# Two-layer convolution block on one core: another order of layer 1's operations on all five engines

## The chip, the core and the metric

The kernel runs on one core of a Trainium2 chip. The metric is the device time of one execution in microseconds (us); lower is better. TensorE (PE) multiplies matrices, VectorE (DVE), ScalarE (ACT) and GpSimd (POOL) work elementwise, and SyncE (SP) issues all the DMAs of the part that is changed. Each engine takes its instructions in program order; they meet through semaphores (`wait_ge`, `then_inc`).

## What is computed

The input x is 4 images of 64 channels by 256 by 256, f32. Each layer adds to x a function of its group norm. Layer 0 (projection, depthwise convolution, patchwise Fourier product, layer norm, projection) is not touched. Layer 1, which is, is cut to this:

```python
xn   = group_norm(x)
r    = einsum('oc,bchw->bohw', w_reduce, xn) + b_reduce        # 64 -> 64
rn   = relu(batch_norm(r))
kern = einsum('kc,bchw->bkhw', w_span, rn) + b_span            # 9 taps for each pixel
inv  = einsum('bkhw,bckhw->bchw', kern, patches_3x3(xn))
z    = softplus(inv)
x    = x + softplus(conv3x3(z, w_conv2) + b_conv2)
```

## The kernel before, in words

Layer 1 runs over 132 strips of 8 image rows. A strip lies as 128 partitions (64 channels, twice, for even and odd rows) by 1024 elements (4 rows of 256). A loop of 33 rounds has four bodies each, k = 0 to 3; the first round is written out, since the first strips have no strips before them. In body k each engine works on several strips at once, as its own hand-written list says. With "strip k" for the body's own strip:

- TensorE, `body` in the block of `pe`. `select(n, b, j)` (line 1309, 2 matmuls) spreads tap n of the kernel values over the 64 channels into one of two PSUM bank pairs; nine for each strip, of which taps 0 and 1 of strip k+1 stand at the end of body k. `r_product` (line 1314, twice) makes r of strip k+2, `weights` (line 1319) its 9 kernel values. `conv(b, h, products)` (line 1327) makes half h of the output convolution from 6 products, the line's records being two for a product. Half 1 has PSUM bank 7, and so do r, the kernel values and `k_rest`: these follow each other in that bank once a strip.
- VectorE. Nine multiplications `prod[n]` (line 1570; tap 7 goes straight to the PSUM pair `b_x`), `add_to_x` (line 1518) adds `prod[8]` and later GpSimd's sum `part_sum` to `b_x`, `z_finish` (line 1528) ends the first softplus, `rest` (1536) and `third_parts` (1541) split the kernel values into three bf16 parts, `residual` (1555, two halves) adds the input to the positive part of the convolution.
- GpSimd. Six additions (line 1292) sum `prod[0]` to `prod[6]` into `part_sum`; one addition (line 1299) makes the output `res`.
- ScalarE. The three normed copies of x, `x_mid` (from `xa`), `x_up` and `x_down` (from `xb`; lines 1397 and 1399), the absolute value, exp and log of both softplus functions, `bn_relu` (1443), the masked edge rows of z (1435, 1437), and two of the bf16 parts (`high_parts` 1451, `second_parts` 1456).
- SyncE. `stack_parts` (1213) writes the three parts to DRAM, `stack_back` (1218, six DMAs) brings them back as `kern_parts`, for `select`; `load_a`, `load_b` (1197 to 1203) load x and `store` (1207) writes the output.

The softplus is computed as max(v,0) + log(1 + exp(-|v|)).

## Time and profile before

| | |
|---|---|
| median of 3 runs | 10036.34 us (10029.1 to 10041.79) |
| profiled execution, its own time | 10034.93 us |
| its span | 10033.1 us, granted TensorE clock 0.988 on the mean |
| layer 1 in it | from about 7440 us to the end |

The trace was read for one strip out of layer 1's steady part, where each strip takes the same time. A row of the timeline has the start in us, the duration, the engine and line, the operation with what it writes and reads, and in brackets the idle time of the engine before it with what ended it. A duration is longer than the distance to the next start on VectorE and ScalarE, since an instruction begins as the one in front drains; a sum over an engine therefore goes by distances between starts.

### The profile page before, as it was taken

Reading aid. Unit: us, or ns where it says so; the run is one execution under the profiler, and the core shown is the slowest. Engines: PE = TensorE matmul, PEld = TensorE weight load, DVE = VectorE, ACT = ScalarE, POOL = GpSimd, SP = SyncE. Lnnn points to the kernel's source line nnn. Section 1 sums busy time; section 2 is a strip of 40 time slices with the busy share of each in tenths; the row PEclk is TensorE's granted clock in tenths of the full one; section 3 lists DMA queues with packets and bytes.
Section 4 is the critical chain, followed back from the end, with each engine's and each line's share of the span. In section 5 each row is a group of like instructions: output and inputs, shape, how many; then the busy total and the mean of one; then the engine's idle time right before and its main releaser. Section 6 shows DMA issues by size and latency. Waiting matters only on the chain. (4 is left out here: it accounts for less than half of the span.)

```text
span 10033.1 us, 169594 instructions
## 1 busy us (share of the span) xinstructions
PE 9128.4 (91%) x58854; PEld 5045.6 (50%) x58854; DVE 6036.7 (60%) x7784; ACT 6973.9 (70%) x9573; POOL 4896.1 (49%) x2751
## 2 busy tenths in 40 slices
PE   1999999999999999999999999999868888888888
PEld 0666666666666666666665555555322222222222
DVE  4555555555555555555555454544558888888887
ACT  1777777777777777777776767767217777777777
POOL 1334433343344344433433333333118888888888
PEclk9999999999999999999999999999989999999999
DMA  6122222222222222222212111111764444444444
GB/s 129 47 60 55 48 57 56 56 50 55 60 55 47 59 56 55 50 55 60 55 39 48 39 48 39 47 40 39 162 157 105 104 104 104 104 104 104 104 104 102
DMA packets 619184, 718.26 MB, mean 72 GB/s; under 512 B 44324, under 2 KB 578138, under 8 KB 595142
## 3 DMA queue, kind: packets, MB, share of 16 engines
q1 hardware_dynamic: 618950, 714.70, 30.2%
q8 instruction: 200, 3.28, 0.1%
q14 instruction: 34, 0.28, 0.0%
HBM read 549.65 MB, written 164.89 MB: 71 GB/s over the span
## 5 line engine op out<-in xcount | busy, mean ns | idle before, releaser
L550 PE MATMUL banks<-w_hi,hi_lo 128*128 128x256 f16 x18432 | 2380.6, 275 | 132.5 <-issue 80.9
L550 PEld LDWEIGHTS banks<-w_hi,hi_lo 128*128 128x128 f16 x18432 | 1795.2, 99 | 556.4 <-issue 209.9
L508 POOL TENSOR_TENSOR u_im<-q_im,k_swap 128x512 f32<-128x512 f32 x512 | 706.4, 1380 | 2136.2 <-ACT q_im L706 2082.8
L1292 POOL TENSOR_TENSOR part_sum<-part_sum,prod 128x1024 f32<-128x1024 f32 x660 | 1559.8, 2363 | 261.7 <-DVE prod L1570 218.8
L1327 PE MATMUL banks<-z,conv_w 128*128 128x512 f32 x3140 | 1523.4, 614 | 0.0
L688 ACT ACTIVATE qk<-banks,inv_wscale 128x512 f32<-128x512 f32 x1024 | 689.9, 687 | 1040.8 <-PE banks L550 1028.4
L818 DVE TENSOR_TENSOR u<-q_re,banks 128x512 f32<-128x512 f32 x512 | 351.0, 686 | 1717.1 <-ACT q_re L712 1341.5
L511 POOL TENSOR_TENSOR u<-u,u_im 128x512 f32<-128x512 f32 x512 | 649.7, 1269 | 1338.8 <-DVE u L818 1338.8
L567 PE MATMUL banks<-hi_lo,w_hi 128*128 128x512 f16 x4608 | 1085.7, 381 | 13.9 <-DVE tmp L887 13.9
L550 PE MATMUL banks<-w_lo_pair,hi_pair 128*128 128x256 f16 x6144 | 1012.0, 274 | 0.0
L498 POOL TENSOR_TENSOR hl_all<-xn,hi_all 64x1280 f16<-64x1280 f32 x258 | 793.2, 3074 | 241.2 <-ACT hi_all L681 219.2
L1327 PEld LDWEIGHTS banks<-z,conv_w 128*128 128x128 f32 x3140 | 540.6, 188 | 613.2 <-issue 613.2
L517 POOL TENSOR_TENSOR u<-u,u_mean 128x512 f32<-128x512 f32 x512 | 532.2, 1039 | 513.4 <-DVE u_mean L833 513.4
L567 PEld LDWEIGHTS banks<-hi_lo,w_hi 128*128 128x128 f16 x4608 | 431.0, 98 | 650.5 <-issue 209.9
L597 PEld LDWEIGHTS banks<-idft,u 128*128 128x128 f32 x4096 | 496.3, 191 | 511.8 <-issue 322.7
L696 ACT ACTIVATE v_s<-banks,inv_wscale 128x512 f32<-128x512 f32 x512 | 349.6, 683 | 546.4 <-PE banks L567 546.4
L675 ACT ACTIVATE xn<-xr,par 128x2816 f32<-128x2816 f32 x129 | 684.0, 5302 | 27.0 <-DMA xr<-in_x_dram 27.0
L1570 DVE TENSOR_TENSOR prod<-banks,x_up 128x1024 f32<-128x1024 f32 x396 | 482.6, 1219 | 313.6 <-PE banks L1309 313.6
L597 PE MATMUL banks<-idft,u 128*128 128x128 f32 x4096 | 594.0, 288 | 73.8 <-POOL u L517 73.8
L550 PEld LDWEIGHTS banks<-w_lo_pair,hi_pair 128*128 128x128 f16 x6144 | 604.3, 98 | 72.6
L1309 PE MATMUL banks<-kern_parts,sel 64*128 64x512 bf16 x2380 | 443.7, 388 | 196.8 <-DVE prod L1570 196.5
L831 DVE TENSOR_REDUCE u_mean<-u 128x4 f32<-128x512 f32 x512 | 351.0, 686 | 434.0 <-POOL u L511 434.0
(210 smaller groups left out, 16400.3 us busy)
## 6 DMA issues: line engine op xcount, KB each, us to landing
xr<-in_x_dram SPq DMA_DIRECT2D x258, 640.0 KB, 9.1
xb<-y_scratch SPq DMA_DIRECT2D x268, 320.0 KB, 4.8
xa<-y_scratch SPq DMA_DIRECT2D x270, 256.0 KB, 5.3
x_res<-in_x_dram SPq DMA_DIRECT2D x258, 256.0 KB, 4.2
out_dram<-res SPq DMA_DIRECT2D x258, 256.0 KB, 5.1
y_scratch<-ys SPq DMA_DIRECT2D x256, 256.0 KB, 4.1
yc<-y_scratch SPq DMA_DIRECT2D x256, 256.0 KB, 6.0
xs<-in_x_dram SPq DMA_DIRECT2D x92, 512.0 KB, 7.1
```

The source lines that it names most:

```text
L498: nc.gpsimd.tensor_tensor(hl_all[C:P, 1 + c0:1 + c1, 1:SL], xn[C:P, c0:c1, 0:SL - 1], hi_all[C:P, 1 + c0:1 + c1, 0:SL - 1], ALU.subtract). ...
L508: nc.gpsimd.tensor_tensor(u_im[:], q_im[:], k_swap[:], ALU.mult).then_inc(u_made, 1)
L511: nc.gpsimd.tensor_tensor(u[:], u[:], u_im[:], ALU.add).then_inc(u_step, 1)
L517: nc.gpsimd.tensor_tensor(u4, u4, u_mean[:].unsqueeze(2).to_broadcast([P, 4, P]), ALU.subtract)\
L550: r = pe.matmul(out, px, w, start=n == 0, stop=n == 13)
L567: r = pe.matmul(b_v[:], w, px, start=n == 0, stop=n == 13)
L597: last = pe.matmul(by_patch[:, p, t], u[:, block], idft[:], start=True, stop=True)
L675: act.activation(xn[:, :, 0:SL], xr[b][:].rearrange("p s w -> p w s"), ACT.Identity, bias=par[b][:, 1:2], scale=par[b][:, 0:1]).then_inc(x ...
L688: act.activation(qk[:, 2 * h:2 * h + 2, :], b_qk[h][:].rearrange("p (t c) -> p t c", t=2), ACT.Copy, scale=inv_wscale[:, 0:1]).then_inc(qk ...
L1292: nc.gpsimd.tensor_tensor(part_sum[:], prod[0][:] if n == 0 else part_sum[:], prod[n + 1][:], ALU.add)\
L1327: last = pe.matmul(b_c[h][:], conv_w[:, n, :], z[b][:, 2 * h + j:2 * h + j + 2, dc:dc + W], start=n == 0, stop=n == 5)
L1570: v.tensor_tensor(by_row(to), by_row(flat(b_kern[(9 * k + n) % 2])), src[:, :, 1 + dc:1 + dc + W], ALU.mult).then_inc(prod_ready, 1)
```

## The change

The set of operations, their sizes and their tiles stay the same. What moves:

- TensorE: the convolution's half 0 is cut into products 0, 1, 2, 3 (each on its own behind a select or another product) and 4, 5; half 1 of the strip before goes from behind select 1 to behind selects 3, 4 and 6 of the next body. Both `r_product` go from behind selects 5 and 6 to behind selects 8 and 0, `weights` to behind select 1.
- VectorE: `rest`, `third_parts` and `add_to_x(prod[8])` go to behind tap 1 of the next body, `residual` to behind taps 4 and 6.
- GpSimd: the output addition of a strip is made one strip later, at the start of a body.
- ScalarE: `second_parts` and `norm_up` go to the front, the rest follows in another order; `norm_up` waits for tap 2 of two strips before instead of for the whole strip before.
- SyncE: the kernel parts that come back in body k are those of strip k+1 (before: k+2); the load of `xa` is that of strip k+2 (before: k+3).

```diff
@@ sync, body
-                        to, of, of_a, of_a1 = (i * 16 + n for n in (4 * (k - 3), 4 * (k + 2), 4 * (k + 3), 4 * (k + 3) + 1))
-                        normed_before, made, given = i * 4 + (k + 2), i * 4 + (k + 3), i * 4 + (k - 1)
+                        to, of, of_a, of_a1 = (i * 16 + n for n in (4 * (k - 3), 4 * (k + 2), 4 * (k + 2), 4 * (k + 2) + 1))
+                        normed_before, made, given = i * 4 + (k + 1), i * 4 + (k + 2), i * 4 + (k - 1)
...
                         sp.wait_ge(mid_normed, normed_before)
-                        load_a(of_a, of_a1, (k + 1) % 2)
+                        load_a(of_a, of_a1, k % 2)
+                        stack_parts(made, k + 1)
                         if not (first and k < 3):
                             sp.wait_ge(out_ready, given_out)
                             store(to, (k + 1) % 2)
-                        stack_parts(made, k)
                         sp.wait_ge(parts_stored, stored)
-                        stack_back(0, (k + 2) % 4)
+                        for h in range(2):
+                            stack_back(h, (k + 1) % 4)
                         if not (first and k < 2):
                             sp.wait_ge(resid_added[1], given)
-                        stack_back(1, (k + 2) % 4)
                         load_b(of, (k + 2) % 4)
@@ gpsimd, body
+                        if not (first and k < 3):
+                            b = (k - 3) % 2
+                            pool.wait_ge(resid_added[0], i * 4 + (k - 2))
+                            pool.wait_ge(resid_added[1], i * 4 + (k - 2))
+                            pool.wait_ge(log2_ready, i * 4 + (k - 2))
+                            nc.gpsimd.tensor_tensor(res[b][:], res[b][:], ab2[b][:], ALU.add).then_inc(out_ready, 1)
                         for n in range(6):
...
-                        if not (first and k < 2):
...
-                            nc.gpsimd.tensor_tensor(res[k % 2][:], res[k % 2][:], ab2[k % 2][:], ALU.add).then_inc(out_ready, 1)
@@ tensor, body
                         for n in range(2, 9):
                             pe.wait_ge(prod_ready, i * 36 + (9 * k + n - 1))
                             select(n, k, 9 * k + n)
-                            if n == 2 and any_2:
+                            if n == 3 and any_2:
+                                conv(b, 0, (4, 5))
+                                pe.wait_ge(third_made, i * 4 + (k + 2))
+                                conv(b, 1, (0,))
+                            if n == 4 and any_2:
+                                conv(b, 1, (1, 2, 3))
+                            if n == 6 and any_2:
                                 conv(b, 1, (4, 5))
-                            if n == 5:
...
-                                r_product((k + 2) % 4, 0)
-                            if n == 6:
-                                pe.wait_ge(rn_ready, i * 8 + (2 * k + 5))
-                                r_product((k + 2) % 4, 1)
                             if n == 7 and any_1:
                                 pe.wait_ge(z_ready, i * 4 + k)
                                 if any_2:
                                     pe.wait_ge(resid_added[0], i * 4 + (k - 1))
                                 conv(1 - b, 0, (0,))
-                            if n == 8:
-                                pe.wait_ge(rn_ready, i * 8 + (2 * k + 6))
-                                weights()
-                                if any_1:
-                                    conv(1 - b, 0, (1, 2))
+                        pe.wait_ge(mid_normed, i * 4 + (k + 3))
+                        if any_2:
+                            pe.wait_ge(resid_added[1], i * 4 + (k - 1))
...
+                        r_product((k + 2) % 4, 0)
+                        if any_1:
+                            conv(1 - b, 0, (1,))
                         pe.wait_ge(prod_ready, i * 36 + (9 * k + 8))
                         pe.wait_ge(parts_stacked[(k + 1) % 2], i * 192 + (48 * (k + 1 - (k + 1) % 2) + 96))
                         select(0, (k + 1) % 4, 9 * k + 9)
-                        if any_1:
-                            conv(1 - b, 0, (3, 4, 5))
+                        pe.wait_ge(rn_ready, i * 8 + (2 * k + 5))
+                        r_product((k + 2) % 4, 1)
                         pe.wait_ge(prod_ready, i * 36 + (9 * k + 9))
                         select(1, (k + 1) % 4, 9 * k + 10)
                         if any_1:
-                            pe.wait_ge(third_made, i * 4 + (k + 3))
-                            conv(1 - b, 1, (0, 1, 2, 3))
+                            conv(1 - b, 0, (2,))
+                        pe.wait_ge(rn_ready, i * 8 + (2 * k + 6))
+                        weights()
+                        if any_1:
+                            conv(1 - b, 0, (3,))
@@ scalar: norm_up, and the order of body
+                        act.wait_ge(prod_ready, (u - 2) * 9 + 3)
+                    norm(u, b, xb[b], 0, x_up[b % 2], 2).then_inc(up_normed, 1)
...
+                        second_parts(u1)
+                        norm_up(u1, b1)
...
+                            z_abs(i, k, any_2)
+                            z_exp(i, k)
...
+                            conv_abs(v, bv, 0, not (first and k < 4))
...
+                            z_log(i, k)
                         params(u2, b2)
                         norm_mid(u2, b2, not (first and k < 2))
...
+                            edge_rows(i, k)
...
+                            conv_abs(v, bv, 1, False)
+                            conv_exp(v, bv)
                         bn_relu(u2, 0)
+                        norm_down(u1, b1)
                         bn_relu(u2, 1)
...
+                            conv_log(v, bv)
                         high_parts(u2, True)
@@ vector, body
+                            if n == 1:
+                                if any_1:
+                                    v.wait_ge(prod_ready, i * 36 + 9 * k)
+                                    add_to_x(prod[8])
+                                rest(i * 4 + (k + 1))
+                                if any_1:
+                                    v.wait_ge(x_step, i * 8 + (2 * k - 1))
+                                    v.wait_ge(pool_step, i * 24 + 6 * k)
+                                    add_to_x(part_sum)
+                                third_parts(i * 4 + (k + 1))
+                            if n == 4:
+                                if any_2:
+                                    residual(i, k, 2, 0)
+                                if any_1:
+                                    z_finish(i, k, any_2)
+                            if n == 6 and any_2:
                                 residual(i, k, 2, 1)
```

## Rows read from the trace of the kernel before

**Rows 1.** The page: busy time by engine.

```profile
PE 9128.4 (91%) x58854; PEld 5045.6 (50%) x58854; DVE 6036.7 (60%) x7784; ACT 6973.9 (70%) x9573; POOL 4896.1 (49%) x2751
```

**Rows 2.** 800 us of layer 1: PE, PEld, DVE, ACT, POOL busy; clock, DMA share, GB/s.

```profile
8400.00:9200.00 800.00, 706.62 (x2235) 235.21 (x2233) 657.07 (x661) 591.74 (x828) 683.14 (x290) 1.00 0.43 104
```

**Rows 3.** Timeline of layer 1's first strips and its last.

```profile
7467.26 0.42 DVE L1541 TENSOR_TENSOR k_parts<-banks,k_parts 128x256 bf16<-128x256 f32 x1 [0.44 <-ACT k_parts L1456]
...
7474.70 1.04 PE L1309 MATMUL banks<-kern_parts,sel 64*128 64x512 bf16 x4
...
7510.83 1.21 DVE L1570 TENSOR_TENSOR prod<-banks,x_up 128x1024 f32<-128x1024 f32 x1
...
10003.51 1.21 DVE L1570 TENSOR_TENSOR prod<-banks,x_up 128x1024 f32<-128x1024 f32 x1
...
10027.87 0.66 SPq L1203 DMA_DIRECT2D xb<-y_scratch  x1
```

**Rows 4.** Timeline of one strip, GpSimd.

```profile
9002.74 2.36 POOL L1292 TENSOR_TENSOR part_sum<-prod 128x1024 f32<-128x1024 f32 x1 [0.38 <-DVE prod L1570]
...
9006.78 12.13 POOL L1292 TENSOR_TENSOR part_sum<-part_sum,prod 128x1024 f32<-128x1024 f32 x5 [1.68 <-DVE prod L1570]
...
9019.32 2.36 POOL L1299 TENSOR_TENSOR res<-res,ab 128x1024 f32<-128x1024 f32 x1 [0.41 <-ACT ab L1470]
```

**Rows 5.** Timeline of the same strip, other engines: around bank 7.

```profile
9005.40 1.22 DVE L1570 TENSOR_TENSOR prod<-banks,x_up 128x1024 f32<-128x1024 f32 x1 [2.16 <-PE banks L1309]
...
9007.22 0.69 ACT L1463 ACTIVATE ab<-banks,conv_b 128x512 f32<-128x512 f32 x1 [0.78 <-PE banks L1327]
9007.64 1.23 DVE L1570 TENSOR_TENSOR prod<-banks,x_mid 128x1024 f32<-128x1024 f32 x1 [1.01 <-PE banks L1309]
...
9008.78 0.74 DVE L1555 SCALAR_TENSOR_TENSOR res<-banks,neg_b,xb 128x512 f32<-128x512 f32 x1
...
9008.92 0.39 PE L1309 MATMUL banks<-kern_parts,sel 64*128 64x512 bf16 x2 [1.20 <-DVE prod L1570]
...
9009.67 1.10 PE L1314 MATMUL banks<-x_mid,wr 128*128 128x512 f32 x2 [0.36 <-DVE res L1555]
...
9011.63 1.13 PE L1314 MATMUL banks<-x_mid,wr 128*128 128x512 f32 x2 [0.54 <-ACT rn L1443]
...
9016.22 0.48 DVE L1536 SCALAR_TENSOR_TENSOR banks<-banks,span_b,k_parts 128x256 f32<-128x256 f32 x1
```

**Rows 6.** The chain that ended last, TensorE's pieces of the same strip: start, us, line.

```profile
9001.32 3.63 PE banks L1327 x8
9004.95 0.32 PE banks L1309 x2
9005.27 1.92 PE banks L1327 x4
...
9013.36 1.05 PE banks L1327 x2
...
9014.74 0.57 PE banks L1319 x8
```

**Rows 7.** ScalarE groups of layer 1 by line: count, busy us, mean ns, idle before.

```profile
L1427 ACT ACTIVATE ab<-ab 128x1024 f32<-128x1024 f32 x116 | 122.6, 1057 | 3.7
L1397 ACT ACTIVATE x_up<-xb,par 128x768 f32<-128x768 f32 x116 | 119.5, 1030 | 115.6 <-DVE prod L1570 59.2 <-DMA xb<-y_scratch 56.4
```

**Rows 8.** Loads of xb by line: us from issue to landing.

```profile
DMA to landing us min/median/max: 4.8/4.9/5.0
```

**Rows 9.** GpSimd additions by line, ns min/median/max: layer 1, then layer 0.

```profile
L1292 POOL TENSOR_TENSOR part_sum<-part_sum,prod x583: 2344/2366/2380, 7697.8 to 9944.0; 128x1024 f32<-128x1024 f32 x195
...
L508 POOL TENSOR_TENSOR u_im<-q_im,k_swap x432: 1261/1270/1752, 1000.9 to 6798.7; 128x512 f32<-128x512 f32 x144
```

More of the change, by code:

```diff
@@ L1142, in build_program @@
             mid_normed = tsem("mid_normed")
-            normed = tsem("normed")
+            up_normed = tsem("up_normed")
+            down_normed = tsem("down_normed")
             r_done = tsem("r_done")
@@ L1254, in _ @@
                     load_b(4 * u, u)
-                for u in range(2):
-                    if u == 0:
-                        sp.wait_ge(mid_normed, 1)
-                        load_a(8, 9, 0)
-                    stack_parts(u + 1, u)
-                    sp.wait_ge(parts_stored, 16 * u + 16)
-                    for h in range(2):
-                        stack_back(h, u)
+                stack_parts(1, 0)
+                sp.wait_ge(parts_stored, 16)
+                for h in range(2):
+                    stack_back(h, 0)
                 run1(sp, body)
@@ L1411, in norm_up, with norm_down @@
                     if not isinstance(u, int) or u >= 2:
+                        act.wait_ge(prod_ready, (u - 2) * 9 + 3)
+                    norm(u, b, xb[b], 0, x_up[b % 2], 2).then_inc(up_normed, 1)
+                def norm_down(u, b):
+                    if not isinstance(u, int) or u >= 2:
                         act.wait_ge(prod_ready, (u - 1) * 9)
-                    norm(u, b, xb[b], 0, x_up[b % 2], 2)
-                def norm_down(u, b):
-                    norm(u, b, xb[b], 1, x_down[b % 2], 3).then_inc(normed, 1)
+                    norm(u, b, xb[b], 1, x_down[b % 2], 3).then_inc(down_normed, 1)
                 def z_abs(i, k, any_before):
@@ L1479, in body @@
                         if any_1:
-                            z_abs(i, k, any_2)
-                            z_log(i, k)
+                            edge_rows(i, k)
                         if any_2:
-                            conv_abs(i * 4 + (k - 2), k % 2, 1, False)
-                        norm_up(u1, b1)
+                            conv_abs(v, bv, 1, False)
+                            conv_exp(v, bv)
                         bn_relu(u2, 0)
-                        if any_1:
-                            edge_rows(i, k)
+                        norm_down(u1, b1)
                         bn_relu(u2, 1)
-                        norm_down(u1, b1)
+                        if any_2:
+                            conv_log(v, bv)
                         high_parts(u2, True)
-                        second_parts(u2)
-                        if any_2:
-                            conv_log(i, k)
-                        if any_1:
-                            conv_abs(i * 4 + (k - 1), (k + 1) % 2, 0, not (first and k < 3))
                 act.add_instruction(mybir.InstLoadActFuncSet(name=nc.get_next_instruction_name(),
@@ L1565, in body @@
                             if n == 0:
-                                v.wait_ge(normed, i * 4 + (k + 1))
+                                v.wait_ge(up_normed, i * 4 + (k + 1))
+                            if n == 6:
+                                v.wait_ge(down_normed, i * 4 + (k + 1))
                             if n < 7 and any_1:
@@ L1571, in body @@
                                             ALU.mult).then_inc(prod_ready, 1)
-                            if n == 0 and any_1:
-                                v.wait_ge(x_step, i * 8 + (2 * k - 1))
-                                v.wait_ge(pool_step, i * 24 + 6 * k)
-                                add_to_x(part_sum)
-                            if n == 1 and any_2:
-                                residual(i, k, 2, 0)
-                            if n == 3 and any_2:
-                                residual(i, k, 2, 1)
-                            if n == 4 and any_1:
-                                z_finish(i, k, any_2)
-                            if n == 8:
-                                rest(i * 4 + (k + 2))
-                        v.wait_ge(prod_ready, i * 36 + (9 * k + 9))
-                        add_to_x(prod[8])
-                        third_parts(i * 4 + (k + 2))
+                            if n == 1:
[3 more added lines that the diff above has]
+                                rest(i * 4 + (k + 1))
+                                if any_1:
+                                    v.wait_ge(x_step, i * 8 + (2 * k - 1))
[3 more added lines that the diff above has]
+                            if n == 4:
+                                if any_2:
+                                    residual(i, k, 2, 0)
+                                if any_1:
+                                    z_finish(i, k, any_2)
+                            if n == 6 and any_2:
+                                residual(i, k, 2, 1)
                 v.wait_ge(zeroed, 2)
@@ L1592, in _ @@
                 v.wait_ge(sel_ready, 2)
-                for u in range(2):
-                    rest(u)
-                    third_parts(u)
+                rest(0)
+                third_parts(0)
                 run1(v, body)
```

36 lines of the change are left out of this document (17 added, 19 removed).

## The prediction

> **What bounds the kernel now.** I read the page first [rows 1]: TensorE is busy 91% of the span, but most of that is layer 0, where nothing changes. So the question is layer 1 alone, and there the view by windows [rows 2] gives the reader a table of limits. Of 800 us TensorE is busy 706.62, GpSimd 683.14, VectorE 657.07, ScalarE 591.74, at the full granted clock. The time of one strip comes from the timeline's first `prod` of strip 2 and of strip 131 [rows 3]: (10003.51 - 7510.83) / 129 = 19.32 us. For each strip that makes TensorE 17.07 us of work, GpSimd 16.50, VectorE 15.87, ScalarE 14.29. Nobody is full: the strip lasts 2.25 us longer than the busiest engine's work, and all of it is waiting of one engine for another.
>
> The timeline of a strip shows where. GpSimd makes its first addition at 9002.74 and then sits until 9006.78, 1.68 us of it idle, because `prod` of tap 2 comes late [rows 4]. VectorE waited 2.16 us for the select of tap 2 before 9005.40 [rows 5], since that select stands behind a run of four convolution products of 3.63 us [rows 6]. Then the debt turns round: VectorE waits 1.01 us for select 3, TensorE 1.20 us for `prod` 3, then 0.36 us for `residual` and 0.54 us for `bn_relu` before the two `r_product` [rows 5]. GpSimd waits 0.41 us for the log before the output addition [rows 4]. So no engine bounds layer 1; the order does. A better order can give at most the way down to the fullest engine.
>
> **The change, step by step.** Nothing is added or removed: 9 selects, 12 products, 2 `r_product`, 1 `weights`; 7 additions on GpSimd; the same on the rest. What a strip costs afterwards is the larger of two things: the fullest engine's work with its unavoidable steps, and the longest ring of dependences.
>
> *TensorE's work.* Runs of 4, 2 and 1 products take 3.63, 1.92 and 1.05 us [rows 6]: 0.86 for each product and 0.2 for entering the run behind a select. A select takes 0.32, `weights` 0.57 [rows 6]. Before, seven of the nine selects are followed by such an entry; the new list has seven too (selects 2 and 5 go straight on to 3 and 6), so cutting the convolution finely costs nothing there. The sum is 14 x 0.86 (12 products and 2 `r_product`, which I take at a product's price: the timeline's 1.13 for the pair of records is a modelled end) + 7 x 0.2 + 9 x 0.32 + 0.57 = 16.9; an entry behind `weights` adds 0.2. So 17.1, as the busy time said 17.07; 16.9 if the second of two adjacent selects is cheaper, 17.3 if entering `weights` from a product costs 0.2.
>
> *GpSimd's work.* Seven additions of 2.36. Five in a chain take 12.13 [rows 4], so a step costs 2.36 and 0.08 between two. With every operand there in time a strip is 7 x 2.44 = 17.1. This is the same figure as TensorE's, by chance; if the waits with three semaphores before the output addition take the 0.41 of before [rows 4] rather than 0.08, it is 17.4.
>
> *Is every operand in time?* I lay the new lists out by hand with t = 0 at `prod` 0 of strip k on VectorE, steps of 1.13 us for a full tile (9008.78 follows 9007.64 by 1.14 [rows 5]), and a `prod` that can start about 0.45 after its select starts (9004.95 to 9005.40 [rows 6, 5]), a select 1.28 after the `prod` two taps before it starts (9007.64 to 9008.92 [rows 5]). TensorE: select 1 at 0.1, product 2, `weights`, product 3, select 2 at 3.1, select 3, products 4 and 5 of half 0, product 0 of half 1 at 5.5, select 4 at 6.4, three products, selects 5 and 6 at 9.6, two products, select 7 at 12.1, product 0, select 8 at 13.5, `r_product` at 13.9, product 1, select 0 at 15.8, `r_product`, select 1 at 17.2. VectorE: `prod` 1 at 0.6, `add_to_x`, `rest` near 3.0, `add_to_x(part_sum)` 3.4, `third_parts` 4.5, `prod` 2 to 4 from 4.9 (they no longer wait for a run of four), `residual` 8.2, `z_finish` 9.3, `prod` 5 and 6 by 11.5, `residual` 12.9, `prod` 7 and 8, done by 16: it has a microsecond over. `third_parts` ends at 5.0 and TensorE wants bank 7 at 5.5. GpSimd's first addition needs `add_to_x(part_sum)`; that runs while GpSimd makes the output addition, whose log is then a whole strip old. This is where its 0.41 goes; and its 1.68 goes since `prod` 2 is there at 6.1, the first addition ends at 8.1. ScalarE: exp and log steps are 1.06, a normed copy's larger part 1.03 [rows 7]; its list reaches the second `conv_abs` at 12.2 just as the bank is ready, after which it has about 1 us to wait for `r_product`. The new place of `z_finish` waits 0.3 for the log, which VectorE can spare.
>
> *The ring of bank 7.* Half 1's six products with three selects between take 6.6 us; `conv_abs` to `residual` 0.85 (0.1 + 0.69 + 0.06, [rows 5]); to `r_product` 0.89, from there to the second one 1.96 [rows 5], the same again to `weights`, its 0.57; 0.91 more to `rest` (15.31 to 16.22 [rows 6, 5]); 1.52 for `rest` and `add_to_x` in front of `third_parts`; 0.5 to the bank's next use. 15.8 us: under 17.1, so it doesn't decide, but only by 1.3.
>
> *The ring through DRAM.* This is new: kernel parts are now split in the body that also selects from them, where before they had a strip more. From `third_parts` by `stack_parts` and six DMAs back to select 0 the chain has 15.8 - 4.5 = 11.3 us. The landing of the six isn't shown, but the start of layer 1 bounds it: `third_parts` began at 7467.26 and the select that reads the parts ran at 7474.70, right behind `weights` [rows 3]: 7.4 us at most, and at least the 0.42 that `third_parts` itself lasts. I take 7.4, the nearest row, with 0.4 for the store of the output, which now stands between: ready at 12.3, with 3.5 to spare. SyncE loads xb at 13.8 and 14.6; they land 4.9 later [rows 8], 2.4 us into the next body, where `norm_up` wants them at about 4. All of this is hidden at nothing; without that cover each microsecond late costs 129 us in all.
>
> The Trainium skill bears on one price here. GPSIMD Engine Reference, section Instruction dispatch, calls about 2.5 cycles for an element the floor of a two-input operation; at the 1.2 GHz of its specifications 1024 elements are 2.1 us, an estimate from the page, against the 2.36 measured [rows 9]. By the page GpSimd would need some 15.5 us for a strip and TensorE alone would bound it; the trace decides, and the two stand level.
>
> *The sum.* A strip at 17.2 us: the level 17.1, and 0.1 because two full engines that also wait for each other don't both stay full. Gain (19.32 - 17.2) x 129 = 273 us. The first two strips save about 4 us (the same walk from 7467). The end: the last loads of xb are issued 24.4 us after the last `prod` 0 (10027.87 - 10003.51) and land 4.9 later [rows 3, 8]; in the new list they are issued at 14.6, but TensorE, ScalarE and GpSimd end at 20 to 20.4, so the tail shrinks from 29.6 to about 21, 8 to 9 us. 10034.9 (the profiled execution's own time, span 10033.1) - 273 - 4 - 8.7 = 9749; the median of the runs is 1.4 above that execution, so 9750.
>
> **Rivals.**
> *A looser fit* (chance 0.22). The walk leaves 0.3 to 0.5 us at `third_parts`, at the edge rows of z and at the second `conv_abs`. If the crossings between engines cost 0.1 to 0.15 more than I read, or GpSimd pays its 0.41 after all, the strip is 17.5 to 17.9: 9790 to 9840. For it: each ring crosses ten times. Against: they were read from the same instructions.
> *GpSimd slowed by VectorE* (0.05). In layer 0 the same kind of addition goes from 1.27 up to 1.75 us [rows 9] while VectorE runs f16 copies. VectorE will be 92% busy instead of 82%. At 8% on each addition GpSimd needs 7 x 2.63 = 18.4: 9905. Against: in layer 1 they stay within 2344 to 2380 ns [rows 9]. The Trainium skill (GPSIMD Engine Reference, Specifications) has the contention with VectorE instructions in a 2-port mode or with two inputs in SBUF; layer 1's all take one from PSUM, and the trace agrees.
> *The trip through DRAM decides* (0.03), the other side. Round that ring a strip lasts the trip plus 5.0 (0.45 to `prod` 0, 4.5 to `third_parts`). It takes the bound over at a trip of 12.2 and makes the kernel slower than before from 14.3; with a trip of 15 the strip is 20.0: +88 us, less the 13 at the two ends, 10110. Against: the measured trip is at most 7.4.
> *The order doesn't matter* (0.02): another wait of 2 us appears for each removed, 19.3 a strip, 10025 to 10040. For it only that five lists interlock.
>
> The forecast itself (a strip at 17.0 to 17.45: 9725 to 9783) has 0.68. The range that leaves out no more than 2 in 10 runs from 9722, TensorE's lower figure, up to 9840, the end of the looser fit. A measurement can tell 0.2%, 20 us, from no change: faster 0.95, within 0.2% 0.02, slower 0.03.
>
> **What would show it.** In 800 us of layer 1 TensorE and GpSimd busy 780 to 795 both; `prod` of `x_up` no longer waiting 2 us for a select; no idle time in front of the output addition; first `prod` 17.2 us apart; select 0 never last released by a DMA. I am wrong if GpSimd's steps show gaps over 0.2, if `conv` of half 1 waits for `third_parts`, if a strip is bound by ScalarE's place of the exp and log, or if the granted clock falls below 1.00 in a fuller TensorE.

## The result and the profile after

| | before | after |
|---|---|---|
| median | 10036.5 us (4 runs, 10029.1 to 10041.79) | 9706.5 us (4 runs, 9705.28 to 9710.04) |
| profiled execution, its own time | 10034.93 us | 9710.04 us |
| its span | 10033.1 us | 9708.2 us |

The ratio is 0.9672, with an interval of 0.9656 to 0.9689. The kernel is faster, as forecast, but by more than forecast: 9706.5 us lies 43 us under the predicted 9750 and 15 us under the low end of the range, 9722.

The page's line of busy time, against [rows 1]:

```profile
PE 9100.9 (94%) x58842; PEld 5020.0 (52%) x58842; DVE 6045.9 (62%) x7781; ACT 6938.6 (71%) x9571; POOL 4887.3 (50%) x2750
```

The same 800 us of layer 1 in the view by windows, against [rows 2] (PE, PEld, DVE, ACT, POOL busy; granted clock, DMA share, GB/s):

```profile
8400.00:9200.00 800.00, 799.96 (x2566) 260.05 (x2564) 757.66 (x759) 665.31 (x947) 781.33 (x333) 1.00 0.53 119
```

TensorE went from 706.62 us of work to 799.96, GpSimd from 683.14 to 781.33, at the same granted clock. TensorE has no idle time left. The 18.7 us in which GpSimd is not busy are short gaps, as its timeline of one strip shows, against [rows 4] (start, duration, engine, line, operation):

```profile
9001.62 2.37 POOL L1296 TENSOR_TENSOR part_sum<-prod 128x1024 f32<-128x1024 f32 x1
9004.07 12.14 POOL L1296 TENSOR_TENSOR part_sum<-part_sum,prod 128x1024 f32<-128x1024 f32 x5
9016.16 2.37 POOL L1289 TENSOR_TENSOR res<-res,ab 128x1024 f32<-128x1024 f32 x1
```

The idle 1.68 us before tap 2 and the 0.41 us before the output addition are gone. Between an addition and the next in the chain there are 0.08 us (9004.07 - 9001.62 - 2.37), but the output addition begins 0.05 us before the chain's record ends (9016.16 against 9016.21).

The chain that ended last, over one strip, against [rows 6] (start, us, engine and line; x counts matmuls, two for a select or a product):

```profile
9002.20 0.32 PE banks L1307 x2
9002.52 2.77 PE banks L1325 x6
9005.29 0.54 PE banks L1307 x4
9005.83 1.92 PE banks L1325 x4
9007.75 0.32 PE banks L1307 x2
9008.07 1.06 PE banks L1325 x2
9009.12 0.32 PE banks L1307 x2
9009.45 1.06 PE banks L1312 x2
9010.50 0.86 PE banks L1325 x2
9011.36 0.32 PE banks L1307 x2
9011.68 1.05 PE banks L1312 x2
9012.74 0.32 PE banks L1307 x2
9013.06 1.06 PE banks L1325 x2
9014.12 0.57 PE banks L1317 x8
9014.68 1.06 PE banks L1325 x2
9015.74 0.54 PE banks L1307 x4
9016.28 2.77 PE banks L1325 x6
```

L1307 is a select, L1325 convolution products, L1312 `r_product`, L1317 `weights`. The chain never leaves TensorE and has no piece "issue": the kernel's time in layer 1 is the sum of this list. From select 4 at 9002.20 to the end of the last piece it is 16.85 us.

The first `prod` of strip 2 and of strip 131, against [rows 3]:

```profile
7510.74 1.23 DVE L1582 TENSOR_TENSOR prod<-banks,x_up 128x1024 f32<-128x1024 f32 x1 [1.66 <-PE banks L1307]
9686.71 2.51 DVE L1582 TENSOR_TENSOR prod<-banks,x_up 128x1024 f32<-128x1024 f32 x2 [0.30 <-PE banks L1307]
```

A strip lasts (9686.71 - 7510.74) / 129 = 16.87 us. The books close on it: 2.455 us less for each of 129 strips is 316.7, the tail after the last of these starts is 9708.2 - 9686.71 = 21.5 instead of 29.6 us, 8.1 less, and 0.1 at the start; together 324.9, which is the difference of the two profiled executions.

The other engines around the points that the prediction had called tight, against [rows 5] (idle time before the instruction and its releaser in brackets):

```profile
9000.51 0.41 DVE L1551 TENSOR_TENSOR k_parts<-banks,k_parts 128x256 bf16<-128x256 f32 x1
9003.44 3.08 SPq L1221 DMA_DIRECT2D kern_parts<-k_stack_scratch  x6
9010.54 0.78 ACT L1447 ACTIVATE rn<-banks,bn_shift,bn_alpha 128x512 f32<-128x512 f32 x1 [0.98 <-PE banks L1312]
9011.29 0.39 PE L1307 MATMUL banks<-kern_parts,sel 64*128 64x512 bf16 x2
```

The parts split at 9000.51 (L1551, `third_parts`) are needed by select 0 at 9011.29 (L1307). The six transfers that bring them back are all issued by 9006.52.

### The profile page after: what moved, and what is told of

Its sections match the earlier page's. It is cut to its first block and busy times, and to the rows that moved or that the text cites. A ratio compares the mean times of both kernels' runs of the same rounds, so it can differ in the third digit from the quotient of the medians.

```text
span 9708.2 us, 169713 instructions
## 1 busy us (share of the span) xinstructions
PE 9100.9 (94%) x58842; PEld 5020.0 (52%) x58842; DVE 6045.9 (62%) x7781; ACT 6938.6 (71%) x9571; POOL 4887.3 (50%) x2750
## 5 line engine op out<-in xcount | busy, mean ns | idle before, releaser
L1325 PE MATMUL banks<-z,conv_w 128*128 128x512 f32 x3128 | 1574.9, 618 | 0.0
L1325 PEld LDWEIGHTS banks<-z,conv_w 128*128 128x128 f32 x3128 | 526.0, 188 | 631.4 <-issue 572.1
L852 DVE TENSOR_TENSOR ys<-ys,t_n 128x512 f32<-128x512 f32 x256 | 593.8, 2319 | 8.7
L783 DVE TENSOR_SCALAR xn<-xn,par 64x256 f32<-64x256 f32 x516 | 209.8, 450 | 574.0 <-ACT xn L675 572.1
```

Of the source, the lines that this page charges most:

```text
L852: v.tensor_tensor(out, out, t_n[:].rearrange("p (c r) -> p r c", r=R), ALU.add).then_inc(fin_step, 1)
L1325: last = pe.matmul(b_c[h][:], conv_w[:, n, :], z[b][:, 2 * h + j:2 * h + j + 2, dc:dc + W], start=n == 0, stop=n == 5)
```

## The experiments

Unless it says otherwise, each is an edit of the changed kernel, and its ratio is to the kernel before. The strip's length is the mean distance between GpSimd's output additions in the steady part, from about 8000 to 9440 us.

### Which engine sets 16.87 us?

TensorE's list and GpSimd's are nearly the same length, so taking work from one alone should give nothing if both bound. Three kernels leave work out.

`e1_pool_light`:

```diff
-nc.gpsimd.tensor_tensor(part_sum[:], ..., prod[n + 1][:], ALU.add)
+w = 512 if n == 5 else 1024
+nc.gpsimd.tensor_tensor(part_sum[:, 0:w], ..., prod[n + 1][:, 0:w], ALU.add)
```

> The changed kernel, but GpSimd's sixth addition of a strip covers 512 of 1024 columns (half of prod[6] is left out of the sum), about 1.1 us less of GpSimd for each strip. Measured strip of the changed kernel: 16.86 us. Theory (TensorE full, its list adds up to 16.87 us without a gap, GpSimd level with it by chance): the strip stays at 16.86, the time within 5 us of 9706. Rival (GpSimd alone is the bound and TensorE is only held up to it): the strip falls towards 15.9, the time by 100 us or more.

Measured: 9703.34 us, 0.967 (0.965 to 0.9689), strip 16.85.

```profile
8400.00:9200.00 800.00, 800.00 (x2567) 261.32 (x2567) 760.36 (x761) 661.52 (x951) 733.97 (x334) 1.00 0.53 120
```

In this window GpSimd has 47 us less to do and the time stays: TensorE holds the strip at 16.85 without it.

`e2_pe_light`:

```diff
                         r_product((k + 2) % 4, 0)
-                        if any_1:
-                            conv(1 - b, 0, (1,))
```

> The changed kernel, but product 1 of the convolution's half 0 is left out, 0.86 us less of TensorE for each strip, nothing else. Theory (both engines level): GpSimd's seven additions hold the strip at 16.8 to 16.9, the time stays within 10 us of 9706. Rival (TensorE alone is full, GpSimd has the room that its small gaps suggest): the strip falls to 16.4 or lower, 9650 or less.

Measured: 9706.62 us, 0.9673 (0.9654 to 0.9692), strip 16.87. TensorE is busy for 776.70 us of the window instead of 799.96, GpSimd for 781.42 as in the changed kernel. So GpSimd holds it without TensorE too.

`e3_both_light` is both edits together.

> Both reductions of the two kernels before together. Theory of two level engines: only now the strip falls, to the next limit: TensorE 16.0, VectorE 16.0 (its work of 757.66 us in 800), so 16.0 to 16.2, about 9600. Rival (a ring of waits holds the strip, not an engine's work): it stays above 16.6.

Measured: 9664.75 us, 0.9631 (0.9612 to 0.9651), strip 16.61. Only with both lightened does the time fall, which shows the level bound; but it falls by 0.26 us a strip and not by the 0.7 to 0.9 that I expected. (That is 33 of the 42 us. Layer 1 also began 15 us earlier in this execution than in the changed kernel's, its first `prod` at 7463.98 against 7479.07 us.) Its chain shows what came next:

```profile
9006.83 1.07 PE banks L1313 x2
...
9007.92 0.79 ACT rn L1446
...
9008.75 1.13 PE banks L1313 x2
```

The product that I left out stood between the two `r_product` (here L1313). It covered `bn_relu` on ScalarE (L1446), which the second `r_product` must wait for since both products write one bank. Without it the chain goes over ScalarE. Below the level a ring holds, and there the rival of this run, a strip above 16.6, has the number right. My expectation missed that the piece left out was a cover as well as a load. The same wait stands in the chain of `e2_pe_light`, but the ring needs only 16.61 us, so what held that kernel at 16.87 was GpSimd.

### Is the second of two adjacent selects cheap?

The forecast had nine selects at 0.32; in the chain above the pairs 2-3 and 5-6 take 0.54 together. `e5_pairs_apart` parts selects 2 and 3:

```diff
+                            if n == 2 and any_2:
+                                conv(b, 0, (4,))
                             if n == 3 and any_2:
-                                conv(b, 0, (4, 5))
+                                conv(b, 0, (5,))
```

> The changed kernel with product 4 of half 0 between selects 2 and 3, so that only one pair of selects is still adjacent. It measures the term that the prediction mis-sized. Theory (the second of two adjacent selects costs 0.22 us instead of 0.32, and each entry into a run of products behind a select 0.2): one entry more and one adjacency less, TensorE's list 17.16 us, the time 9740 to 9748. Rival (adjacent selects save nothing, only the entry counts): 17.06, about 9732. Rival (TensorE isn't the bound): unchanged.

Measured: 9744.39 us, 0.9708 (0.969 to 0.9726), strip 17.16. The chain at that place:

```profile
9001.72 0.32 PE banks L1307 x2
9002.04 1.06 PE banks L1325 x2
9003.10 0.32 PE banks L1307 x2
9003.42 1.91 PE banks L1325 x4
```

3.61 us where the changed kernel has 0.54 + 2.77 = 3.31: 0.1 for the select and 0.2 for one more entry into a run. With 129 strips 0.3 makes 38.7, and the time grew by 37.9. The two prices are confirmed as a sum; no run takes them apart.

### Does making the output addition a strip later pay?

`e4_sum_in_place` puts it back at the end of the body, for the strip whose log has just been made:

```diff
-                        if not (first and k < 3):
-                            b = (k - 3) % 2
...
                         for n in range(6):
...
+                        if not (first and k < 2):
+                            b = k % 2
+                            pool.wait_ge(resid_added[0], i * 4 + (k - 1))
+                            pool.wait_ge(resid_added[1], i * 4 + (k - 1))
+                            pool.wait_ge(log2_ready, i * 4 + (k - 1))
+                            nc.gpsimd.tensor_tensor(res[b][:], res[b][:], ab2[b][:], ALU.add).then_inc(out_ready, 1)
```

> The changed kernel with one part undone: GpSimd's output addition back at the end of the body, for strip k-2 instead of k-3. Theory: in the new ScalarE order the log ends about 1.6 us before GpSimd has its sixth addition done, so the strip later buys nothing: within 5 us of 9706. Rival (the delay of the output sum is what removed GpSimd's wait of 0.41 us): 0.3 to 0.4 us more for each strip, 9745 to 9760.

Measured: 9705.19 us, 0.9671 (0.9654 to 0.9687), strip 16.88. Its timeline has the log (L1475) and the addition that reads it (L1297):

```profile
9023.44 1.05 ACT L1475 ACTIVATE ab<-ab 128x1024 f32<-128x1024 f32 x1
9026.15 2.37 POOL L1297 TENSOR_TENSOR res<-res,ab 128x1024 f32<-128x1024 f32 x1
```

The log ends at 9024.49, 1.7 us before GpSimd comes to the addition. The 0.41 us of [rows 4] had already gone with the new place of the log in ScalarE's list; this part of the change is worth nothing that these runs can tell.

### What is the fine cut of half 1 worth?

`e10_half1_one_run` keeps the new order but makes half 1 one run of six:

```diff
-                                pe.wait_ge(third_made, i * 4 + (k + 2))
-                                conv(b, 1, (0,))
                             if n == 4 and any_2:
-                                conv(b, 1, (1, 2, 3))
-                            if n == 6 and any_2:
-                                conv(b, 1, (4, 5))
+                                pe.wait_ge(third_made, i * 4 + (k + 2))
+                                conv(b, 1, (0, 1, 2, 3, 4, 5))
```

> The changed kernel with one part undone: half 1's six products are one run behind select 4 (before: 1, 3 and 2 of them at three places). TensorE's list gets 0.4 us shorter. Theory (selects 5 and 6 come 2.2 us later, VectorE has 0.9 us to spare): prod 5 and 6, residual and the first r_product are late, a strip of 18.0 to 18.9, 9850 to 9970. Rival (TensorE's sum alone counts): the strip stays at 16.86 by GpSimd, 9706.

Measured: 9906.98 us, 0.9871 (0.9851 to 0.9891), strip 18.45. TensorE around the run:

```profile
9002.19 5.42 PE L1325 MATMUL banks<-z,conv_w 128*128 128x512 f32 x12
9009.34 0.39 PE L1307 MATMUL banks<-kern_parts,sel 64*128 64x512 bf16 x2 [1.20 <-DVE prod L1579]
```

While six products run VectorE gets no tap; from 7700 to 9600 us it waits 255.4 us in all, 206 times, for selects. Then TensorE waits for VectorE (1.20 us). It is the exchange of waits of [rows 5], only larger. 200 of the 330 us are given back.

`e6_before_split` does the reverse: the kernel before, with its run of four and its run of two cut into 2, 2, 2.

```diff
-                            conv(1 - b, 1, (0, 1, 2, 3))
+                            conv(1 - b, 1, (0, 1))
...
                             if n == 2 and any_2:
-                                conv(b, 1, (4, 5))
+                                conv(b, 1, (2, 3))
+                            if n == 3 and any_2:
+                                conv(b, 1, (4, 5))
```

> The kernel before with one part of the change alone: half 1's run of four products behind select 1 is cut into products 0, 1 behind select 1, products 2, 3 behind select 2 and 4, 5 behind select 3. Theory (it is the ring through bank 7 and VectorE's fixed order that sets the strip, so filling VectorE's wait of 2.16 us only moves it): the second r_product starts 0.2 to 0.4 us earlier, the strip goes from 19.32 to 18.9 to 19.2, 9980 to 10025. Rival (the long run is what starves VectorE and GpSimd): a strip of 18.2 or less, 9890 or faster.

Measured: 10016.35 us (8 runs), 0.9979 (0.9969 to 0.9989). It gains 20 us, for two reasons. The first is that the wait moved to the next point of the old order, the first `r_product` (here L1314), which there needs the second `residual` (L1557). The strips that run at the full granted clock last 19.01 us, 0.31 less than before, which would be 40 us. The second is the clock. In the profiled execution (10029.13 us, the slowest of the eight) 24 of 129 strips last 20 to 22 us. The window below is of one of them; in it the granted clock stands at the lower of its two levels (0.50, 1.2 GHz) for about 3 us, right behind TensorE's waits of 1.12 and 0.53 us, and the second `r_product` takes 1.80 us instead of 1.13. The last row is from the view by windows; its third figure from the end is the granted clock:

```profile
9006.54 1.10 PE L1314 MATMUL banks<-x_mid,wr 128*128 128x512 f32 x2 [1.12 <-DVE res L1557]
...
9008.50 1.80 PE L1314 MATMUL banks<-x_mid,wr 128*128 128x512 f32 x2 [0.53 <-ACT rn L1445]
...
9009.00:9010.00 1.00, 1.00 (x2) 0.00 (x0) 1.00 (x2) 0.71 (x2) 1.00 (x1) 0.50 0.00 0
```

The mean granted clock of the eight executions is 0.983 to 0.987, that of the kernel before 0.987 to 0.988. Why it falls here and not in the kernel before, which waits at the same places, no run shows.

So the cut is needed (`e10_half1_one_run`) and not enough. That the later `r_product` is what it lacks is read from this wait; no run moves `r_product` by itself.

### How near are the two rings?

Bank 7. `e8_weights_last` puts product 3 of half 0 in front of `weights` and cuts half 1 into 3 and 3, which takes one entry (0.2 us) off TensorE's list but brings `weights` later:

```diff
                         pe.wait_ge(rn_ready, i * 8 + (2 * k + 6))
-                        weights()
-                        if any_1:
-                            conv(1 - b, 0, (3,))
...
+                        if any_1:
+                            conv(1 - b, 0, (3,))
...
+                        weights()
...
                             if n == 4 and any_2:
-                                conv(b, 1, (1, 2, 3))
+                                pe.wait_ge(third_made, i * 4 + (k + 2))
+                                conv(b, 1, (0, 1, 2))
                             if n == 6 and any_2:
-                                conv(b, 1, (4, 5))
+                                conv(b, 1, (3, 4, 5))
```

> The changed kernel with product 3 of half 0 in front of weights, so that the two products behind select 1 make one run (0.2 us less of TensorE, list 16.67), and half 1 started one select later (products 0 to 2 behind select 4, 3 to 5 behind select 6). Theory: GpSimd, level at 16.86, holds the strip: within 8 us of 9706, with TensorE now idle 0.2 a strip. Rival (the later weights delay third_parts and with it half 1 or the next body): slower by 20 us or more.

Measured: 9855.57 us, 0.9819 (0.9804 to 0.9834), strip 18.02. In its timeline `rest` (L1545) waits for ScalarE's half of the split, VectorE's taps stand behind it, and TensorE then waits for a tap:

```profile
9004.28 0.49 DVE L1545 SCALAR_TENSOR_TENSOR banks<-banks,span_b,k_parts 128x256 f32<-128x256 f32 x1 [0.65 <-ACT k_parts L1454]
9007.42 0.39 PE L1307 MATMUL banks<-kern_parts,sel 64*128 64x512 bf16 x2 [1.26 <-DVE prod L1581]
```

Its chain has `weights` (L1317), select 4 (L1307) and `weights` again:

```profile
9003.14 0.61 PE banks L1317 x8
...
9007.42 0.39 PE banks L1307 x2
...
9021.12 0.61 PE banks L1317 x8
```

The walk gave the ring of bank 7 a slack of 1.3 us, but another ring decides: `rest` and `third_parts` stand in VectorE's list, in front of the taps that TensorE needs. The edit puts two products into it, product 3 in front of `weights` and half 1's first one, which now stands behind select 4. From select 4 to `weights` TensorE takes 13.70 us here and 11.92 in the changed kernel (9002.20 to 9014.12), 1.78 more. From `weights` over `rest`, `third_parts` and `prod` 2 back to select 4 it takes 4.28 us here, without slack, and 4.93 in the changed kernel (9014.12 to 9019.05). By this estimate the changed kernel has 0.65 us to spare in that ring, and 1.78 - 0.65 = 1.13 is nearly the 1.15 us by which the strip grew. Either product alone might already cost time; they were not tested apart.

`e7_tree` asks the same from GpSimd's side. It makes the sum as pairs, (0+1), (2+3), (4+5), so that only the last addition needs the result of the one directly in front (VectorE's waits for free tiles follow the new order; they are not printed here, nor for `e11_two_back`):

```diff
+tree = [(s0, prod[0], prod[1], 2, 0), (s1, prod[2], prod[3], 4, 0), (s2, prod[4], prod[5], 6, 0),
+        (s0, s0, s1, 0, 2), (s2, s2, prod[6], 7, 3), (part_sum, s0, s2, 0, 5)]
```

> The changed kernel with GpSimd's six additions of a strip in another order: three sums of pairs into three tiles, then joined, so that only the last one needs the result of the one directly in front. The same number and size of additions. Theory (an addition that waits for the one in front starts 0.08 us after its end, one that doesn't starts 0.05 before it): GpSimd needs 16.3 to 16.4 us of a strip instead of 16.86 and shows idle time; the strip stays at 16.86, since TensorE is full too: within 8 us of 9706.

Measured: 9787.63 us, 0.9752 (0.9737 to 0.9766), strip 17.53, slower than the changed kernel. Its timeline:

```profile
9007.27 2.37 POOL L1303 TENSOR_TENSOR part<-prod 128x1024 f32<-128x1024 f32 x1 [1.01 <-DVE prod L1588]
9016.89 1.23 DVE L1534 TENSOR_TENSOR banks<-banks,part_sum 128x1024 f32<-128x1024 f32 x1 [1.10 <-POOL part_sum L1303]
9018.50 1.13 PE L1331 MATMUL banks<-z,conv_w 128*128 128x512 f32 x2 [0.37 <-DVE k_parts L1557]
```

The third pair wants `prod` 5 before it is there (1.01 us), so the sum is late, `add_to_x(part_sum)` is late (1.10), and half 1 waits for `third_parts` (0.37). `e9_tree_weights_last` has both edits.

> The two kernels before together: GpSimd at 16.4 and TensorE at 16.67. Theory: neither alone moves the time, both do: a strip of 16.7, 9680 to 9690. Rival (a ring of waits holds it): no change from 9706.

Measured: 9855.28 us, 0.9818 (0.9805 to 0.9832), strip 18.02: what `e8_weights_last` has, so VectorE's list decides there and the tree adds nothing on top.

The way through DRAM. `e12_back_late` brings the second half of the kernel parts back only after the wait for `residual`, as before the change:

```diff
-                        for h in range(2):
-                            stack_back(h, (k + 1) % 4)
+                        stack_back(0, (k + 1) % 4)
                         if not (first and k < 2):
                             sp.wait_ge(resid_added[1], given)
+                        stack_back(1, (k + 1) % 4)
                         load_b(of, (k + 2) % 4)
```

> The changed kernel with SyncE's three DMAs of kern_parts' second half behind the wait for residual, as in the kernel before. It prices the ring through DRAM. Theory: they are issued 5.8 us later than now, the trip from third_parts to select 0 becomes 10.3 us and the landing (unknown, up to 3.0), the strip that trip and 6.1: 17.9 to 19.4, 9840 to 10030, with select 0 released by a DMA. Rival (3.5 us of slack as the prediction had it and a short landing): under 17.2, 9750 or faster.

Measured: 9746.68 us, 0.9711 (0.9692 to 0.9731), strip 17.18. The number is the rival's; of the theory it has that a DMA now releases select 0, in most strips:

```profile
9014.46 0.70 ACT ab L1467
...
9015.18 0.76 DVE res L1565
...
9016.64 1.61 DMA kern_parts<-k_stack_scratch
...
9018.29 0.39 PE banks L1307 x2
```

But the chain does not pass `third_parts`, where the theory had it; that was done at 9007.13. It runs from select 0 (9001.12) along TensorE's list to the end of half 1 (9014.44), over `conv_abs` (L1467), the second `residual` (L1565), the three issues behind it and the last landing back to select 0. So the ring is that of the new wait. The transfer lands 1.6 us after its start, where I had allowed up to 3.0, and the three issues take 1.00 us together. That the wait alone is worth 40 us shows that the early `stack_back` is a needed part of the change.

### Can the level be lowered?

`e11_two_back` keeps GpSimd's additions in the order of the taps, but as two sums that take turns, so that each waits for the addition before the last one:

```diff
+tree = [(s0, prod[0], prod[1], 2, 0), (s1, prod[2], prod[3], 4, 0), (s0, s0, prod[4], 5, 1),
+        (s1, s1, prod[5], 6, 2), (s0, s0, prod[6], 7, 3), (part_sum, s0, s1, 0, 5)]
```

> The changed kernel with GpSimd's six additions in two interleaved sums, so that each needs the result of the one two places in front (only the last also that directly in front), with the products taken in the old order, no later than before. Theory: GpSimd loses 4 of its 5 gaps of 0.08 us and starts each such addition 0.05 us before the one in front ends: 16.4 us instead of 16.86, and it now waits 0.4 us for others; the strip stays at 16.86 because TensorE is full: within 8 us of 9706. Rival (GpSimd is the real bound): 9650 to 9670.

Measured: 9703.56 us, 0.9667 (0.9651 to 0.9683), strip 16.85. Its timeline:

```profile
9015.50 2.37 POOL L1303 TENSOR_TENSOR part<-prod 128x1024 f32<-128x1024 f32 x1 [0.30 <-DVE prod L1588]
9017.83 7.01 POOL L1303 TENSOR_TENSOR part<-part,prod 128x1024 f32<-128x1024 f32 x3
```

Three additions take 7.01 us and start 2.32 apart, less than the 2.37 that one lasts; five chained ones start 2.44 apart in the changed kernel. GpSimd now has 0.30 us to spare before a tap. TensorE holds the strip, so nothing is gained by it alone.

`e16_run_merged` shortens TensorE's list instead, with all work done. Product 2 goes directly behind the second `r_product`, in one run with it, which saves an entry; `add_to_x(prod[8])` goes in front of `prod` 1:

```diff
                         r_product((k + 2) % 4, 1)
+                        if any_1:
+                            conv(1 - b, 0, (2,))
                         pe.wait_ge(prod_ready, i * 36 + (9 * k + 9))
                         select(1, (k + 1) % 4, 9 * k + 10)
-                        if any_1:
-                            conv(1 - b, 0, (2,))
...
+                            if n == 0 and any_1:
+                                v.wait_ge(prod_ready, i * 36 + 9 * k)
+                                add_to_x(prod[8])
                             if n == 1:
-                                if any_1:
-                                    v.wait_ge(prod_ready, i * 36 + 9 * k)
-                                    add_to_x(prod[8])
                                 rest(i * 4 + (k + 1))
```

> The same TensorE and VectorE lists as in the kernel with the interleaved sums, but GpSimd's additions as in the changed kernel. Theory (GpSimd is a limit of its own at 16.86): the strip stays at 16.86, 9698 to 9712, TensorE idle 0.2 a strip. Rival (TensorE alone is the limit): 9678 to 9686 as well.

Measured: 9703.02 us, 0.9667 (0.9652 to 0.9682), strip 16.87: nothing, since GpSimd holds. TensorE is busy for 799.67 us of the window all the same, though its list needs 0.2 us less for a strip: the run that ends with half 1's first product, which waits for `third_parts`, lasts 2.91 us in the chain instead of 2.77. A full busy time by itself therefore does not show that an engine is the bound. `e15_run_merged_two_back` has both edits, and also does all the work:

> The changed kernel with GpSimd's additions in two interleaved sums, and with product 2 of half 0 directly behind the second r_product, so that TensorE enters one run less (list 16.67 us instead of 16.87); select 1 comes later for it, and VectorE makes add_to_x(prod[8]) in front of prod 1 to fill the time. All work is done. Theory (the entry of 0.2 us is the term, and weights comes no later, so bank 7's ring isn't stretched): a strip of 16.65 to 16.7, 9678 to 9686. Rival (the ring of bank 7 or VectorE's list holds the strip at 16.86 whatever TensorE's list is): 9700 to 9710.

Measured: 9680.5 us (5 runs, 9677.65 to 9681.93), 0.9645 (0.9632 to 0.9658), strip 16.66. It beats both kernels. Its chain shows the merged run and the saved 0.2:

```profile
9009.13 1.06 PE banks L1318 x2
9010.19 0.86 PE banks L1331 x2
```

The four kernels `e1`, `e2`, `e16` and `e11` each lighten one of the two lists and leave the strip at 16.85 to 16.87; `e3` and `e15`, which lighten both, shorten it. That is the form of a level bound. (`e9` lightens both too, but lengthens the ring through VectorE's list.)

## Why the prediction was right in kind and 43 us off in size

**Right: the order bounded, and the change takes the strip down to the fullest engine.** Waits of some 2 us for a select and of 1.68 and 0.41 us on GpSimd are gone, TensorE is full, and GpSimd is level with it. The forecast of 780 to 795 us busy was right for GpSimd (781.33) and low for TensorE (799.96). The tail gave 8.1 us against 8 to 9. Select 0 is not released by a DMA; the last of the six transfers starts near 9006.2 (three issues take 1.00 us in `e12_back_late`) and lands 1.6 later, which leaves 3.5 us before select 0, as predicted. ScalarE waits 0.98 us for `r_product`, against "about 1".

**Wrong: the term "a strip at 17.2".** It is 16.87, and 0.33 x 129 = 43 us is the miss: 9750 - 43 = 9707. Three pieces of it were mis-sized, all upward.

- TensorE's list. I took 17.1 and named 16.9 for the case that the second of two adjacent selects is cheaper. It is: a pair takes 0.54, not 0.64, and there are two pairs. The list is 14 x 0.86 + 8 x 0.2 + 7 x 0.32 + 2 x 0.22 + 0.57 = 16.89, where the chain has 16.85. `e5_pairs_apart` shows the price.
- GpSimd's list. I put 0.08 us behind each of seven additions, 17.1 in all. Only five hand-overs, where an addition needs the result just made, cost that; the two around the output addition don't depend on their neighbour and overlap it by some 0.05. 7 x 2.37 + 5 x 0.08 - 2 x 0.05 = 16.9. `e2_pe_light` shows the bound, `e11_two_back` shows that the 0.08 goes when the dependence goes.
- The 0.1 for "two full engines that also wait for each other". It costs nothing: the chain has no gap.

The price of a pair of selects stood in the timeline of the kernel before, in the very strip that I had read:

```profile
9007.12 0.60 PE L1309 MATMUL banks<-kern_parts,sel 64*128 64x512 bf16 x4
```

Two selects last 0.60 us there and one lasts 0.39 [rows 5], so the second adds 0.21. I passed over it, because the busy time ran to 17.07 and my sum of 17.1 agreed with it. That agreement was chance. By the same prices the old list, where selects 3, 4 and 5 stand together, is 14 x 0.86 + 7 x 0.2 + 7 x 0.32 + 2 x 0.22 + 0.57 = 16.69. My count of entries was wrong as well: before, six of the nine selects, not seven, are followed by one, and a seventh stands behind `weights`; the new list has seven and one. So the fine cut does cost an entry, 0.2 us a strip, and `e15_run_merged_two_back` takes that back.

**Small things.** The start gave 3.4 us where I had 4: from layer 1's first `r_product` (7456.14 us, before 7452.86) to the first `prod` of strip 2 it takes 54.60 us instead of 57.97. It doesn't show in the total, because layer 1 itself began 3.3 us later in this execution. The low end of the range was a slip as well: it was called TensorE's lower figure, but a strip of 16.9 makes 9711, not 9722. And the slack of bank 7, 1.3 us, was read off its own ring alone; the ring through VectorE's list has only some 0.65, as `e8_weights_last` shows.

**The rivals.** GpSimd isn't slowed by VectorE: with VectorE busy for 757.66 us of 800 a chained addition still takes 2345 to 2382 ns with a median of 2364, against 2344 to 2380 in [rows 9]. The Trainium skill (GPSIMD Engine Reference, section Instruction dispatch) would have an addition at about 2.1 us by its floor, an estimate from the page; no run here comes near, and `e11_two_back` with starts 2.32 us apart is the closest. The looser fit didn't come, though `e7_tree` (17.53) and `e8_weights_last` (18.02) show how near an order that looks as good lies to it. The trip through DRAM doesn't decide, but it does as soon as it has one more wait in it (`e12_back_late`). And the order did matter, by 2.45 us a strip.

**What each part is worth.** The cut of half 1 carries 200 us within the new order and 20 alone (40 at the full granted clock); the early return of the parts 40; the output addition a strip later nothing measurable. How the rest divides between the later `r_product`, ScalarE's order and VectorE's wasn't taken apart and stays open.

## What to carry to other kernels

When no engine is full, add up each engine's list with its entry and hand-over prices, from rows of the same neighbourhood, and take the largest as the floor. Don't let the busy time confirm the sum: it can hold waits (`e16_run_merged`). And keep the uncertainty two-sided, since two lists that stood level here cost nothing extra for it. To test a level bound lighten one engine, then the other, then both, and look at what the piece left out was covering. A reordering pays as a set: undoing the cut or the earlier transfer took 200 or 40 us back, and the cut alone gave 20.

## What the runs showed of the hardware

- On GpSimd an addition that needs the result of the one just in front starts 0.08 us after its end; one that doesn't starts 0.05 us before its end (2.44 against 2.32 us apart, `e11_two_back`).
- Of two adjacent bf16 selects on TensorE the second takes 0.22 us, where one between f32 products takes 0.32, and the f32 run behind a select costs 0.2 us to enter (`e5_pairs_apart`: 0.3 us for one of each together).
- The transfer of kernel parts from DRAM lands 1.6 us after its start (`e12_back_late`). The six issues of a strip take 3.08 us on SyncE's queue in the changed kernel; why one of them takes some 1 us is open.
- In the strip of `e6_before_split` shown above the granted clock fell to its lower level (0.50) for some 3 us, behind waits of TensorE of 1.12 and 0.53 us, and the strip took 20.39 us instead of 19.01; in the changed kernel, where TensorE doesn't wait, it stood at 1.00 from 7600 to 9600 us.
